# Dense adjacency blocks of a graph kernel: in pass 0 VectorE adds one column of a tile and ScalarE copies eleven, over one PSUM pair and two block buffers, with three gather slots

## What is computed

```python
agg = segment_sum(x[src], dst)                      # pass 0
h1 = (agg + x) @ W1 + b1                            # 256 -> 1024
h1 = relu(batchnorm_over_nodes(h1))
x = layernorm(x + relu(h1 @ W2 + b2))
for W, b in three layers:                           # passes 1 to 3
    h = relu(segment_sum(norm * (h @ W.T)[src], dst) + b)
x = layernorm(x + h)
```

## Time and profile before

| | |
|---|---|
| time, median of 3 runs | 2933.99 us (2928.63 to 2935.6) |
| span of the profiled execution | 2930.2 us |
| PE busy / DVE / ACT / POOL over the span | 82% / 49% / 33% / 69% |
| TensorE clock granted, mean | 0.919 |
| gathers of pass 0, first and last start | 11.6 and 1088.0 us |
| stretch behind pass 0 | from about 1115 us |

### The profile page before, as it was taken

How to read it: one execution, slowest core, us unless ns; L and a number is a source line. 1 busy time by engine, 2 the same in 40 slices (tenths; PEclk the granted TensorE clock), 3 DMA queues, 4 the chain that set the end, 5 groups by cost and what they waited for, 6 DMA issues and landing times.

```text
span 2930.2 us, 44233 instructions
## 1 busy us (share of the span) xinstructions
PE 2390.3 (82%) x15784; PEld 1770.1 (60%) x15784; DVE 1427.8 (49%) x3556; ACT 956.0 (33%) x1512; POOL 2020.2 (69%) x2141
## 2 busy tenths in 40 slices
PE   3676666766666678999999987899998889999986
PEld 2444444444444447776777765677776667777754
DVE  7787777678677775760223233122222321424234
ACT  0111111111111115554444433444444334344431
POOL 6777777777777760017777777677777757777774
PEclk9988878888878888999999999999999999999998
DMA  4444554555454446987889898779898977888894
GB/s 136 141 159 143 162 161 141 161 160 161 143 160 159 144 148 219 344 305 251 296 297 308 285 330 297 242 255 307 298 311 297 312 235 245 298 275 285 272 315 127
DMA packets 360951, 680.17 MB, mean 232 GB/s; under 512 B 44051, under 2 KB 190441, under 8 KB 354827
## 3 DMA queue, kind: packets, MB, share of 16 engines
q0 software_dynamic: 102576, 295.31, 32.3%
q10 hardware_dynamic: 154688, 222.02, 22.6%
q1 hardware_dynamic: 103451, 159.81, 15.4%
HBM read 559.42 MB, written 117.51 MB: 231 GB/s over the span
## 4 chain that ended last, share of the span: by engine, by line
PE 60%; DVE 17%; DMA 9%; issue 7%; DVEq 2%; ACT 2%; POOL 0%; SPq 0%; ACTq 0%; POOLq 0%
PE ps L1074 30%; PE ps L938 8%; PE ps L976 6%; PE ps L920 6%; DVE vreg L1263 5%; PE ps L986 4%; DMA hbuf<-parts_d 4%; DMA xs<-in_x_dram 3%; PE ps L950 2%; DVEq L1220 2%; DVE vreg L1250 1%; DVE vreg L1244 1%; PE ps L963 1%; DMA xs<-x_d 1%; ACT strips L679 1%
## 5 line engine op out<-in xcount | busy, mean ns | idle before, releaser
L632 POOL DMA_INDIRECT ring<-table_d,idx x1236 | 1183.6, 958 | 437.7 <-issue 375.4
L1074 PE MATMUL ps<-wide,hbuf 128*128 128x512 f32 x4116 | 1039.7, 404 | 38.0 <-DMA hbuf<-parts_d 32.1
L632 POOL DMA_INDIRECT ring<-in_x_dram,idx x832 | 821.0, 987 | 264.0 <-issue 251.6
L1074 PEld LDWEIGHTS ps<-wide,hbuf 128*128 128x128 f32 x4116 | 760.4, 191 | 262.5 <-issue 60.7
L792 ACT CAST wide<-abuf 128x1024 fp32r<-128x1024 uint8 (+1 forms) x588 | 552.5, 940 | 633.3 <-PE ps L1074 632.6
L1216 DVE TENSOR_TENSOR acc<-acc,ps 128x256 f32 x260 | 107.5, 413 | 663.8 <-PE ps L938 662.5
L920 PE MATMUL ps<-ring,hot 128*32 128x256 f32 x4136 | 317.4, 429 | 101.1 <-issue 82.7
L950 PE MATMUL ps<-vreg 128*128 128x300 bf16 x840 | 197.3, 345 | 231.0 <-DVE vreg L1263 212.2
L938 PE MATMUL ps<-place,strips 128*128 128x128 f32 x2068 | 317.9, 303 | 64.7 <-ACT strips L679 34.6
L938 PEld LDWEIGHTS ps<-place,strips 128*128 128x128 f32 x2068 | 295.1, 214 | 105.9 <-ACT strips L679 55.8
L1263 DVE TENSOR_TENSOR vreg<-vreg,ps 128x600 f32 x420 | 329.4, 784 | 54.4 <-DVE vreg L1263 23.6
(11 more groups left out here) (131 smaller groups left out, 1541.2 us busy)
## 6 DMA issues: line engine op xcount, KB each, us to landing
hbuf<-parts_d ACTq DMA_DIRECT2D x84, 1024.0 KB
hbuf<-parts_d ACTq DMA_DIRECT2D x84, 768.0 KB
abuf<-ad_d ACTq DMA_DIRECT2D x63, 896.0 KB
parts_d<-vreg SPq DMA_DIRECT2D x72, 512.0 KB, 7.2
h_d<-ureg SPq DMA_DIRECT2D x23, 1024.0 KB, 7.3
ureg<-h_d POOLq DMA_DIRECT2D x23, 1024.0 KB, 8.2
ad_d<-vreg SPq DMA_DIRECT2D x28, 784.0 KB, 4.2
ring<-table_d,idx POOLq DMA_INDIRECT x1236, 4.9
```

The costliest lines, as they stand in the source:

```text
L632: pool.indirect_dma_start(out=ring[:, i % SLOTS, j, :], out_offset=None, in_=table[0:N, :], in_offset=at).then_inc(g["rows"][i % SLOTS], 16)
L1074: ins = pe.matmul(ps[:, 2 + 4 * q + h, 0:(n1 - 4 * q) * P].rearrange("p (s n) -> p s n", n=P), hbuf[:, bl, e * D + h * P:e * D + (h + 1) * P],
```

## The change

The program is rewritten around one list, `PLAN`, that every engine walks. It can also take part of pass 0 from dense blocks, but `HALFRUNS = 0` leaves that part empty: no "part", "dense", "lstrips" or "lsums" is ever in the list. What is left:

- `ring` has three slots in pass 0 (`SLOTS0`), four in the later passes.
- The 420 tiles are spread evenly over groups 2 to 102 (4 or 5 to a group), and within a group between its other work.
- DVE makes `lohot` for two tiles at once, as a TENSOR_TENSOR; TB is 4.
- There is one pair of PSUM banks for the tiles. `build(t)` waits for both engines that read tile t - 1.
- DVE adds the first column of the tile's 12 (50 elements) to the block. Then ACT copies the other eleven (550 elements) over what stands there. Places are read into registers five at a time, on both engines.
- There are two `ablk`; ACT clears the next one in the middle of a block.
- `hs` uses one half for all chunks but the last but one, and a chunk waits for the store of the chunk before.

```diff
+HALFRUNS = 0
+SLOTS0 = 3
...
+    BEGIN = 2
+    TURN = NS0 // 2 if HALFRUNS else BEGIN
+    TILES_AT = [a + b for a, b in zip(spread(range(TILES0), BEGIN, TURN), spread(range(TILES0, NT), TURN, NS0 - 1))]
...
+        more = [("part", c, 0) for c in PARTS_AT[s]] + [("tile", t, 0) for t in TILES_AT[s]]
+        behind = [[] for _ in work]
+        for n, m in enumerate(more):
+            behind[(2 * n + 1) * len(work) // (2 * len(more))].append(m)
+        PLAN.append([x for w, ms in zip(work, behind) for x in (w, *ms)])
...
-        TB = 6
+        TB = 4
...
-        ablk = part(vreg, NBP * P // 4).bitcast(U8).rearrange("p (b n) -> p b n", n=P)
+        aclear = [part(vreg, NBP * P // 4) for _ in range(2)]
+        ablk = [t.bitcast(U8).rearrange("p (b n) -> p b n", n=P) for t in aclear]
...
+                    slots = SLOTS if a else SLOTS0
+                    if i >= slots:
+                        pool.wait_ge(g["strip"], place_in_line(a, i - slots) + 1)
...
+            def keep_hidden(s, r, pr):
+                v, n = hidden_half(r), size(ORDER0[r])
+                if pr == 0 and v == 0:
+                    wait(act, s["hst"], 16 * min(r, NCH - 1))
...
+            def clear_block(g):
+                wait(act, s_bst, (g - 1) * 16)
+                act.copy(aclear[g % 2], zeros[:, 0:1].to_broadcast([P, NBP * P // 4])).then_inc(s_bz, 1)
+
+            def keep_tile(t, starts):
+                g = max(g for g in range(NS) if FIRST[g] <= t)
...
+                act.wait_ge(s_ba, t + 1)
+                wait(act, s_bc, t)
+                act.copy(ablk[g % 2][:, :, bass.ds(starts[t % READ] + 1, SPAN - 1)].rearrange("p (e b) n -> p e b n", e=2),
+                         tile_bank(SPAN)[:, :, :, 1:SPAN]).then_inc(s_bc, 1)
+                if t == FIRST[g] + SUPER // 2 and g + 1 < NS:
+                    clear_block(g + 1)
...
             def build(t):
                 pe.wait_ge(s_oh, t + 1)
-                wait(pe, s_ba, t - 1)
+                wait(pe, s_ba, t)
+                wait(pe, s_bc, t)
...
             def tile_hot(t):
                 at, j = t // TILES, t % TILES
-                wait(dve, s_bm, t - TB + 1)
-                dve.tensor_scalar(lohot[:, t % TB, :], iotal, lot[:, at, j:j + 1], None, ALU.is_equal)
+                wait(dve, s_bm, t - TB + 2 - t % 2)
+                if t % 2 == 0:
+                    dve.tensor_tensor(lohot[:, t % TB:t % TB + 2, :], lot[:, at, j:j + 2].unsqueeze(2).to_broadcast([P, 2, P]),
+                                      iotal.unsqueeze(1).to_broadcast([P, 2, P]), ALU.is_equal)
                 dve.tensor_scalar(jhot[:, t % TB, :], iotaj, keyt[:, at, j:j + 1], None, ALU.is_equal).then_inc(s_oh, 1)
...
+            def add_tile(t, starts):
...
                 dve.wait_ge(s_bm, t + 1)
                 wait(dve, s_ba, t)
...
-                to = ablk[:, :, bass.ds(off, SPAN)].rearrange("p (e b) n -> p e b n", e=2)
...
-                dve.tensor_tensor(to, to, tile, ALU.add).then_inc(s_ba, 1)
...
+                wait(dve, s_bc, t)
+                to = ablk[g % 2][:, :, bass.ds(starts[t % READ], 1)].rearrange("p (e b) n -> p e b n", e=2)
+                dve.tensor_tensor(to, to, tile_bank(SPAN)[:, :, :, 0:1], ALU.add).then_inc(s_ba, 1)
```

More of the change, by code:

```diff
@@ L158, in gnn_kernel @@
-    BUILD_AT = [a + b for a, b in zip(EARLY_AT, LATE_AT)]
-    assert sum(BUILD_AT, []) == list(range(NT))
+    assert sorted(ORDER0) == sorted(ORDER1) == list(range(NCH + 1)) and ORDER0[-1] == NCH
+    TURN0 = {c: r for r, c in enumerate(ORDER0)}
+    FIRST = [T0[d] + g * SUPER for d in range(ND) for g in range(NSG[d])]
+    LAST = [T0[d] + min(DT[d], (g + 1) * SUPER) - 1 for d in range(ND) for g in range(NSG[d])]
+    assert sum(TILES_AT, []) == list(range(NT))
+    READ = 5
+    PARTS_AT = [list(range(3 * s - 3, min(3 * s, NCH + 1))) if HALFRUNS and s else [] for s in range(NS0)]
@@ new lines, in gnn_kernel, with one_step @@
+    assert not HALFRUNS or (sum(PARTS_AT, []) == list(range(NCH + 1)) and not any(PARTS_AT[READY0 - 1:]))
+    PLAN = []
+    for s in range(NS0):
+        steps = iter(STEPS0[s])
+        def one_step():
+            return [("dense", k, 0) for k in itertools.islice(steps, 1)]
+        work = [("strips", s, 0)] + [("own", TURN0[c], 0) for c in AT0[s][:1]] + one_step() + [("sums", s, 0)]
+        work += [("lstrips", s, 0)] * len(LIGHT_AT[s]) + one_step() + [("lsums", s, 0)] * len(LIGHT_AT[s])
+        for c in AT0[s]:
+            if c != AT0[s][0]:
+                work.append(("own", TURN0[c], 0))
+            for pr in range(HP):
+                work += [("hidden", TURN0[c], pr)] + one_step()
+        work += [("dense", k, 0) for k in steps]
+        more = [("part", c, 0) for c in PARTS_AT[s]] + [("tile", t, 0) for t in TILES_AT[s]]
[3 more added lines that the diff above has]
+        PLAN.append([x for w, ms in zip(work, behind) for x in (w, *ms)])
@@ L336, in gnn_kernel @@
         s_ba = sem("s_ba")
+        s_bc = sem("s_bc")
         s_bz = sem("s_bz")
@@ L377, in gnn_kernel @@
         NCH1 = NCH + 1
-        STATS_AT = list(range(NG - 2 - HT, NG - 2))
-        WELL = max(sum(AT0[:STATS_AT[0]], [])) + 1
+        STATS_AT = list(range(NS0 - 2 - HT, NS0 - 2))
+        WELL = len(sum(AT0[:STATS_AT[0]], []))
         EVEN, ODD = NCH // 2 + 1, NCH // 2
@@ new lines, in keep_tile @@
+            def keep_tile(t, starts):
+                g = max(g for g in range(NS) if FIRST[g] <= t)
+                if t == FIRST[g]:
+                    act.wait_ge(s_bz, g + 1)
+                if t == 0:
+                    act.wait_ge(s_pad, 32)
+                if t % READ == 0:
+                    n = min(READ, NT - t)
+                    _, starts[:] = nc.values_load_multi_w_load_instructions(
+                        offs[0:1, t:t + n], [mybir.EngineType.Activation], min_val=0, max_val=P - SPAN,
+                        skip_runtime_bounds_check_because="the row is cut to these bounds where it is made")
+                act.wait_ge(s_ba, t + 1)
[4 more added lines that the diff above has]
+                    clear_block(g + 1)
@@ L750, in _ @@
             act.wait_ge(s_srcst, 16)
-            for k in EVERY:
-                keep_strips(0, k)
-                if k == 0:
-                    act.wait_ge(s_kt, 2)
-                if k == 2:
-                    flag = regular(act)
-                for c in AT0[k]:
-                    keep_hidden(fast[0], c)
+            starts = []
+            for i, work in enumerate(PLAN):
+                if i == BEGIN:
+                    flag = regular(act)
+                    clear_block(0)
+                for what, n, pr in work:
+                    if what == "strips":
+                        keep_strips(0, n)
+                    if what == "lstrips":
+                        keep_counts(n)
+                    if what == "tile":
+                        keep_tile(n, starts)
+                    if what == "dense":
+                        for k in range(2 if n else 0, 3) if n else range(3):
+                            if n + k < NSTEP0:
+                                widen0(n + k)
+                    if what == "hidden":
+                        keep_hidden(fast[0], n, pr)
             with act.If(flag < 1):
@@ new lines, in add_quad @@
+            def add_quad(j, n):
+                starts = columns(bases, FIRST0[j], QUAD, N - 1)
+                dve.wait_ge(aggs[0]["acc"], n)
+                dve.wait_ge(s_step0, (j + 1) * NB)
+                for m, g in enumerate([*range(0, QUAD, 2), *range(1, QUAD, 2)]):
+                    if g == 1:
+                        dve.wait_ge(s_dacc0, QUAD * j + m)
+                    to = acc[:, :, bass.ds(starts[g], P)]
+                    dve.tensor_tensor(to, to, ps[:, 6:8, g * P:(g + 1) * P], ALU.add).then_inc(s_dacc0, 1)
+                dve.wait_ge(s_dacc0, QUAD * (j + 1))
```

503 lines of the change are left out of this document (328 added, 175 removed).

## The result

The changed kernel takes 3076.3 us (median of 4 runs, 3064.7 to 3083.9) where the kernel before takes 2933.4 beside it: a ratio of 1.049, 95% interval 1.046 to 1.052. That is **142.9 us more**; forecast were 43, and the range ended at 3030. The profiled execution has a span of 3071.3 us.

The account below looks back on a forecast made before the run. The prediction took POOL's gathers to bound pass 0. With the change PE's chain would set the pace: 1016 + 25 + 14, together 1055 us against 1012.8, so 43 us on 2934 gave 2977 us, range 2908 to 3030.

Parts of the forecast that it names:

- What bounds pass 0 before: Pass 0 of the kernel before is as long as POOL's 730 gathers, 10.30 us for a group of eight.
- POOL would wait for PE: Sign in pass 0: POOL's gathers wait for PE's counts some 40 us or more; the last starts near 1130 us.
- DVE's relief: Pass 0: adding one column instead of all, and dropping the clears, saves DVE time but is worth 0.
- ACT's work: Pass 0: ACT's 420 copies of 0.62 us each, 260 us together, cost 0 as work.
- The tail: Pass 0, between tiles on PE: DVE's column, ACT's copy and hand-overs take 1.2 us before the next tile.
- The group's sum: PE's chain in pass 0: 8.25 us for a plain group of four tiles, 16.2 us with a chunk.
- the clock: PE in pass 0: granted clock kept at 0.83, read as two thirds of the time at the higher level.
- Rival A: Pass 0: POOL stays the bound and its gathers get shorter, 25 us less, 2909 us; chance 0.22.
- The room of 1.2 us: Pass 0 of the kernel before: PE, DVE and ACT together had some 1.2 us to spare in a group.
- Register reads in fives: Pass 0, DVE and ACT: reading tile places into registers five at a time was put at 0.
- Rival C: Pass 0: the chain is longer, with a tail of 1.6 us, 3054 us; chance of beyond 3020 us 0.10.
- The rule on rotating banks: PE's tiles in pass 0: taken at its word every tail is bare, 182 us more; the prediction set it aside.

Follow-up runs that it names:

- e2: The changed kernel with two PSUM pairs for the tiles in place of one, register reads still in fives: 2934.2 us, ratio 1.000 to the kernel before.
- e3: The changed kernel with two PSUM pairs and registers read one at a time: 2933.3 us, ratio 1.000 to the kernel before.
- e16: The changed kernel with four unused matmuls on PE ahead of each tile that follows another, reads in fives: 2971.8 us, ratio 1.012 to the kernel before.
- e1: The changed kernel with DVE and ACT reading registers one at a time in place of five: 3028.4 us, ratio 1.031 to the kernel before.
- e18: The kernel before with one PSUM pair for its tiles in place of two: 3104.1 us, ratio 1.058 to the unedited kernel before.
- e13: The changed kernel itself, run again in a job where the kernel before took 3594 us: 3585 us.

## Why the prediction was wrong

**What bounds pass 0 before, and that POOL would wait for PE: right.** POOL's waits for 1102 are 141.7 us ("some 40 us or more" was named), and the last gather starts at 1213 us instead of 1130. In e2 and e3 POOL's pace is back to the microsecond.

**That DVE's relief is worth 0 and ACT's work costs 0 as work: right** (e2 has both and stands at the kernel before), and behind pass 0 nothing moved.

**The tail: right in kind, 1.38 us for 1.2.** Two terms were off, and the hand-overs came out shorter by 0.03 in sum. DVE's column takes 375 ns, not 0.20 (bounds 0.17 to 0.27): "about 1 ns for one more" does not carry over to 50 elements that lie 128 bytes apart. Whether it is the distance, the bytes or the read from PSUM, no run tells. ACT's copy takes 676 ns in the mean, not 0.62. The group's sum was sound nevertheless: with the half-clock terms (strips 2.10, tile 0.66, sums 2.21) it gives 2.10 + 0.66 + 1.2 + 0.66 + 2.21 + 2.5 + 0.66 = 9.99 us, and the group above took 9.77.

**The step that failed is the clock.** The prediction put "A mean of 0.83 is two thirds of the time at the higher level" under a chain that it had itself given new gaps. The clock fell to 0.70, and for the same work PE's busy time rose by 87 us. The same sum with 0.70 in place of 0.83, two fifths of the time at the higher level, has strips at 1.73 us, sums at 1.87 and a tile at 0.56: 8.98 us for a plain group, and 17.2 for one with a chunk (with pairs and transposes longer as measured, 416 ns for 405 and 411 for 362). That is about 1135 us from group 3 to 103, where 1055 were forecast and 1154 measured: an estimate by which the clock is 80 of the 99 us that were missing. e16 shows the other side: with the gaps filled the changed kernel takes 2972 us. That this is so near the forecast of 2977 is in part luck, since the clock was 0.90 there and not 0.83, and the reads in fives still cost something. Rival A spoke of the clock as what decides, but only upwards. The point at which to look was the chain's own feedback: longer tails, lower clock, longer matmuls, a longer chain.

The room of 1.2 us in a group was read too high for the same reason: the 9.1 us a group from 86 to 259 us were taken at a clock of 0.88, and the groups behind them ran at 0.82. The sum itself does not use it.

**Register reads in fives at 0: wrong.** They cost 48 us (e1), since a read of five takes 1.19 us in the median and stands in front of the column and the copy. The prediction put them at nothing without a reason, and counted neither their length nor what waits for one. Rival C named them with "a tenth here and there". Its 3054 us are the nearest figure of the prediction, at a chance of 0.10, but for a partly wrong reason: it wanted a tail of 1.6 us at the old clock, and the plain tail is 1.38 at a lower one.

**Three slots, TB 4, two blocks, one half of `hs`: 0, right** where POOL sets the pace: e2 keeps them all and stands at the kernel before.

**The rule on rotating banks** (the Trainium skill, Perfetto Trace Analysis, section Optimizing Tensor Performance, Matmuls: independent groups of matmuls should go through different PSUM banks in turn, so that one is read while the next is made) was weighed by me at 182 us on top of my 43, and set aside. Rotating the pairs gave back 142 us (e2), taking the rotation from the kernel before cost 170 (e18). The runs agree with the rule; the page has no size. My 43 was 100 us too low and the 225 some 80 too high. That tails with other work behind them are covered, which I held against the 182, is true too; what was missing came through the clock, and the reads.

**Rival A's shorter gathers** hardly came: the longest gather is 1655 ns for 2332, the mean 969 for 983, and in e2, where POOL sets the pace, the kernel is not faster. Rival A drew on the Trainium skill (SBUF — State Buffer, Who interferes with whom), by which a VectorE instruction that holds the shared port pair blocks GpSimd for as long as it lasts. Rows 7 bear that out less than the prediction said: the long gather ends at 936.37, 1.5 us behind the last one-hot at 934.88, and a gather takes 0.95 us otherwise.

## What to carry to other kernels

Before a hand-over is put between engines, look at what stands behind it: one buffer pair taken away from a producer cost 142 us here, and a split of one 785 ns add into 375 + 676 ns on two engines, with the second engine's register reads, cost 112 behind that one pair, although both engines had room; with two pairs it cost nothing. When a forecast lengthens TensorE's gaps, the clock must not be taken from the profile before: sum the chain at both clock levels and take the lower one as the other end. Read registers one at a time, ahead of a wait, where an engine waits anyway; a read of several stands as one block in front of whatever needs the first of them.

## What the runs showed of the hardware

- The granted clock does not follow the busy share: 644 of 960 us busy at 0.83 before, 637 at 0.70 in the changed kernel, 608 at 0.76 in e18. Nor does it follow the idle time: from 150 to 1080 us PE is idle for 304 us before, in gaps of which 46 last 1.2 to 3 us, and for 312 us in the changed kernel, in 152 of these; in e1, at 0.74, no gap is longer than 2.9 us. What sets the clock is not settled here.
- Work without a use, 147 groups of four matmuls in 930 us, raised the clock from 0.70 to 0.90 (pass 0, e16): 114.5 us of filler in the gaps, and 104 us less in the end.
- A read of five register values takes 1.19 us in the median, one value 0.30; the longest took 3.8 us.
- DVE adds 50 elements out of PSUM to bytes that lie 128 apart in 375 ns, and 600 in 784. ACT's copies of 550 fall into two kinds: 301 of the 420 took 0.6 to 0.7 us and 119 took 0.76 to 0.84; why is open.
- Three times, on two chips, the kernel before took 3600 us and all engines of a core paused together again and again. In e13 there are 91 stretches over 0.8 us in which no engine works, half of them of 1.3 to 1.8 us and many some 12 us apart; they add up to 157 us, where e13 takes 509 us more than the changed kernel did undisturbed. Every variant with one pair in the new order took 3575 to 3588 us there. What paused the engines, and what the rest of the time is, was not found.
